# A decoder's first cross attention: the add to x moved between the adapter's maximum and the adapter's shift

## The reference, cut to what matters

```python
scores = jnp.einsum('bhqd,bhkd->bhqk', q, k) * inv_sqrt_d
scores = jnp.maximum(scores + attention_mask, jnp.finfo(scores.dtype).min)
w = jax.nn.softmax(scores, axis=-1)
attn_output = jnp.einsum('bhqk,bhkd->bhqd', w, v)
a_scores = jnp.einsum('bhqd,bhkd->bhqk', q, a_k) * inv_sqrt_d
a_scores = jnp.tanh(gate) * jax.nn.softmax(a_scores, axis=-1)
attn_output = attn_output + jnp.einsum('bhqk,bhkd->bhqd', a_scores, a_v)
return attn_output @ Wo          # and x = x + this
```

## Time and profile before

| what | value |
|---|---|
| three runs | 6960.28, 6961.89, 6986.48 us; median 6961.89 |
| profiled execution, span | 6964.3 us, of which the stage is about 440 to 1335 us |
| busy over the whole span | TensorE 83%, VectorE 73%, ScalarE 54%, GpSimd 45% |
| mean granted clock of TensorE | 0.938 of full speed |
| one tile of the stage, add to add | 25.8 and 26.0 us in turn, in some tiles 27.5 to 27.7 us |

### The profile page before, as it was taken

One profiled execution on the slowest core, in us unless ns is written; L12 is line 12 of the kernel. 1 busy time (PEld: TensorE's weight loads), 2 busy tenths in 40 slices (PEclk: granted clock), 3 DMA queues, 4 the chain that ended last, 5 costly groups with the idle time before them and its releaser, 6 DMA issues. The chain is left out here.

```text
span 6964.3 us, 201035 instructions
## 1 busy us (share of the span) xinstructions
PE 5747.8 (83%) x68832; PEld 4031.1 (58%) x68833; DVE 5091.3 (73%) x11259; ACT 3753.1 (54%) x7483; POOL 3102.7 (45%) x5159
## 2 busy tenths in 40 slices
PE   5878999879377888888888888888888888688584
PEld 4757888645135555555555555655555555577342
DVE  6966777652357888888888888888888888655564
ACT  2324444302146767666666767676666767477121
POOL 2320000130336666666666666666666666400403
PEclk9989999889689999999999999999999999899697
DMA  1000000112300000000000000000000000001213
GB/s 34 0 17 6 5 5 5 43 49 81 86 18 15 13 16 16 13 16 13 16 13 16 13 16 15 14 16 13 16 13 16 13 16 14 10 13 35 100 63 102
DMA packets 137622, 172.75 MB, mean 25 GB/s; under 512 B 29104, under 2 KB 112144, under 8 KB 136720
## 3 DMA queue, kind: packets, MB, share of 16 engines
q1 hardware_dynamic: 125200, 137.43, 6.4%
q0 software_dynamic: 12288, 33.57, 1.5%
HBM read 128.74 MB, written 42.21 MB: 25 GB/s over the span
## 5 line engine op out<-in xcount | busy, mean ns | idle before, releaser
L2519 DVE TENSOR_TENSOR d_kq<-d_qkv,d_pre 128x512 f32<-128x512 f32 x768 | 567.0, 738 | 207.8 <-ACT d_pre L2743 207.8
L2484 DVE SCALAR_TENSOR_TENSOR d_y<-d_ps_kv,d_head,d_y 128x504 f32<-128x504 f32 (+2 forms) x768 | 561.8, 732 | 53.0 <-ACT d_y L2697 34.6
L2857 PE MATMUL d_ps_kv<-d_xnT,d_wqkv 128*128 (+1 forms) x1024 | 545.9, 659 | 38.4 <-issue 16.6
L1589 POOL MEMSET m_earlier<- 128x64 f32 x2 | 0.3, 152 | 1262.9 <-POOLq L3084 1262.9
L2945 PE MATMUL d_ps_tx<-d_T,d_W 64*64 64x64 f32 x10240 | 447.8, 228 | 107.1 <-ACT d_T L2689 107.1
L2945 PEld LDWEIGHTS d_ps_tx<-d_T,d_W 64*64 64x64 f32 x10240 | 365.9, 138 | 189.1 <-issue 160.1
L2935 PEld LDWEIGHTS d_ps_tx<-d_W,d_NT 64*64 64x64 f32 x10240 | 349.6, 134 | 208.5 <-issue 206.2
L2345 POOL TENSOR_TENSOR d_roots<-d_radicand,d_power 128x20 f32<-128x20 f32 x128 | 459.3, 3588 | 10.0
L2922 PE MATMUL d_ps_level<-d_kq,d_ks 128*64 128x64 f32 x10240 | 441.4, 229 | 0.7 <-ACT d_vT L2660 0.7
L2935 PE MATMUL d_ps_tx<-d_W,d_NT 64*64 64x64 f32 x10240 | 437.8, 225 | 2.7 <-DVE d_W L2566 2.7
L2689 ACT COPY d_T<-d_ps_tx 128x128 f32<-128x128 f32 x640 | 169.8, 265 | 458.3 <-PE d_ps_tx L2935 455.3
(11 more groups left out here) (461 smaller groups left out, 16669.7 us busy)
## 6 DMA issues: line engine op xcount, KB each, us to landing
d_wqkv<-in_d_wqkv SPq DMA_DIRECT2D x128, 384.0 KB, 3.1
m_xg<-m_rows_in SPq DMA_DIRECT2D x144, 128.0 KB, 2.0
m_rows_out<-m_ye SPq DMA_DIRECT2D x144, 128.0 KB, 1.7
b_ctx<-in_ctx SPq DMA_DIRECT2D x64, 128.0 KB, 2.0
d_wg<-in_d_wg SPq DMA_DIRECT2D x128, 64.0 KB, 2.6
x_sb<-in_x SPq DMA_DIRECT2D x8, 512.0 KB, 7.5
m_wgu<-in_m_wgu SPq DMA_DIRECT2D x2, 2048.0 KB
out<-x_sb SPq DMA_DIRECT2D x8, 512.0 KB, 3.5
```

The lines of the kernel that those rows point to most:

```text
L2484: ins = nc.vector.scalar_tensor_tensor(out3, in3, head[A.i][:, tap:tap + 1], out3, ALU.mult, ALU.add)
L2519: nc.vector.tensor_tensor(dst, src, by, ALU.mult).then_inc(sems["kq_ready"], 1)
L2857: last = nc.tensor.matmul(ps_qkv[j], wqkv[u.i][:, j, kt, :], xnT[:, kt, tokens(u)], start=(kt == 0), stop=(kt == KT - 1))
```

## The change

`shift_adapter` is cut in two. `adapter_maximum(C)` waits for the adapter scores and takes the maximum; `shift_adapter(C)` keeps the wait for room in the buffer (p1_ps), the wait for the maximum and the shift. Between the two VectorE now runs `add_out(D)`, which waits for the out projection (y_ps). The instructions are the same, and so are those of the other engines.

```diff
+                def adapter_maximum(u):
+                    dve.wait_ge(sems["adapter_ps"], u.n)
+                    m3 = mx[ADAPTER][:, :].rearrange("p (c r) -> p c r", r=PER)
+                    nc.vector.tensor_reduce(m3, by_heads(ps_s), AX.X, ALU.max).then_inc(sems["adapter_max"], 1)
+
                 def shift_adapter(u):
-                    dve.wait_ge(sems["adapter_ps"], u.n)
                     wait_positive(dve, sems["p1_ps"], u.n * 4 - 8)
                     m3 = mx[ADAPTER][:, :].rearrange("p (c r) -> p c r", r=PER)
-                    nc.vector.tensor_reduce(m3, by_heads(ps_s), AX.X, ALU.max).then_inc(sems["adapter_max"], 1)
                     dve.wait_ge(sems["adapter_max"], u.n)
...
                     if C:
                         self_probs_out(C, 1)
+                        adapter_maximum(C)
+                    if D:
+                        add_out(D)
+                    if C:
                         shift_adapter(C)
-                    if D:
-                        add_out(D)
```

More of the change, by code:

```diff
@@ L771, in vector_step @@
                         self_probs_out(C, 1)
-                        shift_adapter(C)
+                        adapter_maximum(C)
                     if D:
                         add_out(D)
+                    if C:
+                        shift_adapter(C)
                 tile_steps(dve, vector_step, TILES, 4)
```

## The result

The changed kernel takes 7082.35 us (median of 5 runs, 7074.71 to 7083.39) against 6968.59 us (5 runs of the kernel before, 6960.28 to 6986.48): a ratio of 1.0162 with a 95% interval of 1.0150 to 1.0174. It is 114 us slower, 1.6%, where 6988 us were forecast. The direction and the two waits behind it were the forecast's; the size was more than four times as large.

The account below looks back on a forecast made before the run. No engine was the limit everywhere; in the first cross attention two chains reach the self scores almost together. Terms 8 - 12 + 27 + 3 = +26 us gave 6990 us on the profiled execution, forecast 6988 us, range 6958 to 7008.

Parts of the forecast that it names:

- the two chains: Before the self scores: add, values, probabilities on one side; shift, exponential, key copy on the other; said to arrive almost together.
- the gain of 1.1 us: TensorE's wait before the values goes, so it reaches the self scores about 1.1 us earlier.
- The shift later: VectorE's shift starts 0.34 us later behind the add, delaying the self scores 0.28 us in each of 30 tiles: +8 us.
- The seven old drops gone: Seven TensorE clock drops behind the idling before the values vanish, 1.7 us each: -12 us.
- The drops at the new place: TensorE's clock drops behind the new idling before the self scores in 18 tiles, 1.5 us each: +27 us.
- rival three: Clock drops come at almost every tile before the self scores: +44 us, 7006 us; chance 0.16.
- The add as a block: On VectorE the add waits for a late out projection, holding up the shift, in two tiles, 1.3 us each: +3 us.
- Rival two: Clock drops vanish, none before the self scores: -4 us, about 6959 us with one blocked add; chance 0.10.

Follow-up runs that it names:

- the idling moved back: Changed kernel with one wait added on TensorE: the values also wait for the tile's adapter shift; 6998.9 us, 1.0044 of the kernel before.
- more filling: Changed kernel with TensorE computing the first sequence's values twice and two of the four last transposes twice; 6990.5 us, 1.0031 of the kernel before.
- the first filling: Changed kernel with TensorE computing the first sequence's values of a tile twice, 0.94 us more work; 6998.8 us, 1.0043 of the kernel before.

## Why the prediction was wrong

What the time rests on was seen: the two chains that reach the scores together, the key copy as the later one, the gain of 1.1 us that turns into idling ahead of the scores, and the clock that falls behind it. Term by term, against the 105 us of the 29 tiles:

- **The shift later, +8.** Right. The shift starts 0.34 us later for the add alone (1182.82 to 1183.16), and the scores follow a copy that ends last by 0.29 us (1187.87 to 1188.16; bounds were 0.24 and 0.32). The two rows from which the prediction took its 0.34 us are multiplications and not adds, as it calls them; the value held. Clean tiles of 26.2 to 26.3 us with the idling moved back, for 25.9 before, bear the term out.
- **The seven old drops gone, -12.** Right. No low stretch begins at the values any more; the last row of the table has -14.0, of which the two hundredths to a tenth per tile between key copy and scores are the rest.
- **The drops at the new place, +27 (ends 0 and 45).** This is the step that failed: "I take 18, the middle between 7 and 30", at 1.5 us each. There were 29 in 30 tiles, 23 of them twice as long as any in the steady tiles before (6.8 us and not 3.4), and with +15.3 and +60.3 they cost 75.6 us, 2.6 each. The number was rival three's. The price held for a short one: four tiles that have only a short low stretch behind the self scores take 27.5 to 27.7 us, the one tile without any 26.35. The one with only a long stretch takes 29.3. The upper end was too low because the price was taken from a stretch of 3.4 us and held for all.
- **The add as a block, +3 (0 to 8).** The other step that failed. Low stretches behind the adapter's scores were two in the kernel before and 24 in this one; VectorE's wait at the add is 45.8 less 29 x 0.34 = 36 us. The mechanism and its price per tile (1.5 us seen, 1.3 forecast) were right, its number was taken from the kernel before.

The second number was taken as if the falls behind the adapter's scores kept the rate of the kernel before. In the changed kernel they go along with the long stretches: of the 22 tiles with a long low stretch behind the self scores (the last tile's scores left out), 21 have one behind the adapter's scores as well, and of six with a short one, two. Whether the first brings the second is not shown, since with more filling 14 tiles have the second kind and three the first. Nor does the second bring the next one of the first kind by making the idling ahead of the self scores longer, as one might think (timelines between 931 and 960 us):

```profile
940.53 0.42 DVE L750 TENSOR_TENSOR x_sb<-x_sb,b_ps_b 128x256 f32 x1 [0.19 <-PE b_ps_b L1045]
```
```profile
945.86 2.71 PE L976 MATMUL b_ps_s<-b_kT,b_qT 16*128 16x64 f32 x64 [1.54 <-ACT b_kT L804]
```

In this tile of the changed kernel nothing falls behind the adapter's scores and the add hardly waits, yet TensorE idles for 1.54 us, as in the tile shown above, and a long low stretch follows. Over the stage the idling is 1.45 to 1.54 us in the six tiles without a fall behind the adapter's scores, 1.24 to 1.54 in the 24 with one. It is 1.45 us in the one tile without any low stretch, so it was longer than the forecast 1.2 to 1.4 us without a drop's help. Even rival three with its 7006 us was less than half of it. How long a drop lasts, and whether one kind comes with the other, should have been cases of their own, and the range open upwards.

The Trainium skill, "TensorE: Matmul & The Clock Gate", section "Why this matters for your kernels", names only long idle gaps between bursts of matmuls as what brings the lower clock back. The traces disagree: behind 1.24 to 1.54 us of idling ahead of the self scores the clock fell in 29 of 30 tiles. Rival two, for which that rule would have spoken, had 6959 us.

What stays open: why a gap ahead of the self scores, which are small 16-row matmuls, brings the clock down more often than one ahead of the values. That it does is shown by moving the gap, and by the first filling, whose shorter gap there brought it down as often as a longer one ahead of the values; what of the scores or of the work around them does it is not. Open, too, is why 23 stretches were long. None of that kind stood in the steady tiles of a kernel whose gap ahead of the self scores was 0.67 us or less. And why fuller work ahead of the self scores left 14 low stretches behind the adapter's scores, where the first filling had 7.

## What to carry to other kernels

Where two chains reach an instruction within a few tenths of a microsecond, taking the wait from one only moves the idling to the other: shorten both in one step, as the key copy ahead of the exponential does here. Before TensorE's idling is moved, look at what stands behind its new place; the granted clock row of one tile tells more than the length of the gap. A clock drop on the critical cycle can come in nearly every tile and last twice as long as any seen before: bound such a term by its worst case in every tile, in number and in length, and not by what the kernel before shows.

## What the runs showed of the hardware that was not expected

Work that nobody needs (0.94 us a tile) and a wait that nobody needs each made the changed kernel some 83 us faster. A stage that was at 1.00 or 0.99 of full speed in most of its stretches of 20 us spent a third of its steady tiles at 1.2 GHz (10 of 30.6 us) with the same instructions in almost the same order.
